# A gather of table rows by matmul, split in two exact float32r parts, with late gathers written out one by one, in a graph-network layer

## The reference

```python
xs = x[src]                                       # a row of x for each edge
deg_w = jnp.maximum(seg(edge_weights), 1.0)
deg_c = jnp.maximum(seg(jnp.ones_like(edge_weights)), 1.0)
norm = edge_weights / jnp.sqrt(deg_w[src] * deg_w[dst])
gcn = seg(norm[:, None] * xs) @ Wgcn + bgcn
sage = x @ Wsage_s + seg(xs) / deg_c[:, None] @ Wsage_n + bsage
agg_w = seg(edge_weights[:, None] * xs)
gin = ((1.0 + gin_eps) * x + agg_w) @ Wgin + bgin
gconv = x @ Wgc1 + agg_w @ Wgc2 + bgc
eop = seg(edge_weights[:, None] * jax.nn.relu(xs + edge_attr)) @ Wedge + bedge
out = layernorm(x + einsum('k,knd->nd', weights, stack([gcn, sage, gin, gconv, eop])))
```

## Time and profile before

| | |
|---|---|
| median of three runs | 2072.93 us |
| the profiled execution: span from first to last instruction | 2149.6 us |
| PE busy | 1612.0 us (75%) |
| POOL busy | 1416.1 us (66%) |
| DVE busy | 949.9 us (44%) |
| ACT busy | 868.5 us (40%) |
| mean granted TensorE clock | 0.891 |

### The profile page before, as it was taken

The page is one execution under the profiler, slowest core; times in us unless marked ns, Lnnn a source line. Parts: engine busy times, 40 slices in busy tenths (PEclk is TensorE's granted clock), DMA queues, the critical chain, the costliest instruction groups (busy, mean ns, idle before and its releaser), DMA issues.

```text
span 2149.6 us, 24142 instructions
## 1 busy us (share of the span) xinstructions
PE 1612.0 (75%) x6229; PEld 1037.0 (48%) x6229; DVE 949.9 (44%) x2579; ACT 868.5 (40%) x1181; POOL 1416.1 (66%) x1730
## 2 busy tenths in 40 slices
PE   2006577688889888888888988978988888888435
PEld 1005567545445454555455545545545455445335
DVE  7882465534334343443244433433435253334325
ACT  3784333334434252543254433533435253344003
POOL 6673766676676667667767666666666666666761
PEclk9999865889999899999899998989989999999757
DMA  5111433322222222222222222221222222212421
GB/s 98 25 25 46 132 106 100 83 44 47 58 51 61 48 47 58 52 48 58 44 66 49 55 60 44 54 51 43 68 48 47 54 57 47 59 43 56 103 44 37
DMA packets 81242, 124.52 MB, mean 58 GB/s; under 512 B 28856, under 2 KB 30631, under 8 KB 80009
## 3 DMA queue, kind: packets, MB, share of 16 engines
q0 software_dynamic: 44544, 48.32, 13.4%
q1 hardware_dynamic: 34966, 74.37, 10.9%
q10 hardware_dynamic: 1650, 1.04, 0.2%
HBM read 120.23 MB, written 3.40 MB: 58 GB/s over the span
## 4 chain that ended last, share of the span: by engine, by line
PE 40%; issue 20%; another core or an unknown queue 17%; DVE 11%; ACT 6%; POOL 3%; DVEq 2%; DMA 0%; POOLq 0%; SPq 0%; ACTq 0%
PE psum L1276 26%; PE psum L1257 11%; ACT ring L606 4%; POOL ring L564 3%; DVE ring L1072 2%; DVE sums L1061 2%; DVE early L986 1%; ACT early_x L687 1%; DVE attr L951 1%; DVE early L990 1%; PE psum L1308 1%; PE psum L1337 1%; PE psum L1338 1%; DVEq L1061 1%
## 5 line engine op out<-in xcount | busy, mean ns | idle before, releaser
L564 POOL DMA_INDIRECT ring<-node_table,idx x1280 | 1239.5, 968 | 612.4 <-issue 505.3
L1276 PE MATMUL psum<-table_sb,early_x 128*128 128x455 f32 x2464 | 1040.0, 572 | 46.5 <-issue 33.3
L1276 PEld LDWEIGHTS psum<-table_sb,early_x 128*128 128x128 f32 x2464 | 479.4, 200 | 531.2 <-issue 516.4
L1257 PE MATMUL psum<-ring 128*128 128x120 f32 x2560 | 412.5, 316 | 225.2 <-DVE ring L1072 104.7
L1257 PEld LDWEIGHTS psum<-ring 128*128 128x128 f32 x2560 | 378.3, 226 | 289.8 <-issue 160.1
L687 ACT ACTIVATE early_x<-early,minus_ids 128x256 f32<-128x256 f16 x616 | 408.1, 746 | 239.2 <-remote 144.6
L986 DVE TENSOR_TENSOR early<-psum,digit_hot 128x455 f32<-128x455 f32 x176 | 111.0, 631 | 885.4 <-remote 580.8
L678 ACT ACTIVATE early<-early 128x256 f32<-128x256 f32 x44 | 18.3, 416 | 523.4 <-DVE early L1007 305.0
L653 ACT ACTIVATE ring<-attr 128x512 f32<-128x512 f32 x160 | 99.6, 623 | 319.2 <-DVE attr L951 230.6
L690 ACT ACTIVATE early_x<-early_x,ones 128x1792 f32<-128x1792 f32 x88 | 157.4, 1789 | 2.9
L1257 PE MATMUL psum<-early 128*128 128x120 f32 x576 | 100.8, 328 | 75.8 <-issue 37.0
(11 more groups left out here) (156 smaller groups left out, 611.3 us busy)
## 6 DMA issues: line engine op xcount, KB each, us to landing
attr<-in_edge_attr SPq DMA_DIRECT2D x79, 512.0 KB
ring<-node_table,idx POOLq DMA_INDIRECT x1280
early<-in_edge_attr SPq DMA_DIRECT2D x36, 256.0 KB
src_all<-in_src SPq DMA_DIRECT2D x7, 1024.0 KB
early<-key_rows SPq DMA_DIRECT2D x11, 512.0 KB
early_x<-degree_rows SPq DMA_DIRECT2D x2, 1568.0 KB
early_x<-in_x,early_idx POOLq DMA_INDIRECT x112
node_table<-table_sb SPq DMA_DIRECT2D x1, 1666.0 KB, 6.1
```

The costliest lines, as they stand in the source:

```text
L564: nc.gpsimd.indirect_dma_start(out=feat[:, u, j, D:BLOCK], out_offset=None, in_=table, in_offset=bass.IndirectOffsetOnAxis(ap=idx[:, u, j: ...
L1257: last = nc.tensor.matmul(to[:, 0:3 * WINDOW], features[:, j, 0:2 * D], hots[:, j].rearrange("p k n -> p (k n)"), start=(j == 0), stop=(j ...
L1276: last = nc.tensor.matmul(pick_ps[k % 2].rearrange("p (b c) -> p b c", b=SPLIT), node_hot[:, k, a], table_sb[:, a * SPLIT:(a + 1) * SPLIT, ...
```

## The change

1. The node table is split by DVE into two parts whose sum is exactly the table: `table_hi` keeps each number's upper bits (the lower 12 are masked off), `table_lo` is the rest. Both, and the one-hot `node_hot`, are of type float32r. `pick_tile` issues 14 matmuls of 128x462 in place of seven of 128x455. 
2. `table_sb` no longer has its own memory: it lies in `sums[:, 1]`. So `sums[:, 1]` is set to zero only after the table is stored, split and lifted, and not at the start of the kernel.
3. The keys are stored tile by tile, so that ACT reads them for a tile as a row (`keys_of`), and the activation that makes them (L617) writes them in that order.
4. POOL's late gathers are written out as 160 times 8 instructions without a loop, and read their indices in `e_src`. The copies to `idx` and the waits for them are gone. 
5. The memory that the compiler is given for the descriptors of POOL's DMAs, `dynamic_dma_scratch_size`, is set to 4096 bytes of a partition; before, it was left at its default.

```diff
-        table_sb = sb("table_sb", [P, NT, TROW])
-
-        idx = sb("idx", [P, UNROLL, TILES], U32)
-
+        table_sb = sums[:, 1, 0:NT * TROW].rearrange("p (t d) -> p t d", d=TROW)
+        table_hi, table_lo = (sb(name, [P, NT, PART], F32R) for name in ("table_hi", "table_lo"))
+        top = ring[:, FEATS:FEATS + NT * PART].rearrange("p (t d) -> p t d", d=PART)
...
-        keys_of = [key_all[:, k * CHUNK:(k + 1) * CHUNK].rearrange("p (e j) -> p j e", j=TILES) for k in range(TURN_CHUNKS)]
+        keys_of = [key_all[:, k * CHUNK:(k + 1) * CHUNK].rearrange("p (j e) -> p j e", e=P) for k in range(TURN_CHUNKS)]
...
                 pool.wait_ge(table_stored, 16)
-                with pool.Fori(0, LATE_STEPS) as i:
-                    for u in range(UNROLL):
-                        it = v * LATE + i * UNROLL + u
-                        pool.wait_ge(gathered[u], (v * LATE_STEPS + i) * (16 * TILES))
-                        for j in range(TILES):
-                            if j % HALF == 0:
-                                tiles = slice(j, j + HALF)
-                                nc.gpsimd.tensor_copy(idx[:, u, tiles], e_src[:, bass.ds(i * UNROLL + u + BASE, 1), tiles].rearrange("p c j -> p (c j)")).then_inc(staged, 1)
-                                pool.wait_ge(staged, it * 2 + j // HALF + 1)
-                                if j == 0:
-                                    pool.wait_ge(chunk_product, it + 1)
-                                pool.sem_inc(gathers_begun, 1)
-                            nc.gpsimd.indirect_dma_start(
-                                out=feat[:, u, j, D:BLOCK], out_offset=None, in_=table,
-                                in_offset=bass.IndirectOffsetOnAxis(ap=idx[:, u, j:j + 1], axis=0),
-                            ).then_inc(gathered[u], 16)
+                for c in range(LATE):
+                    u = c % UNROLL
+                    if c >= UNROLL:
+                        pool.wait_ge(gathered[u], (v * LATE_STEPS + c // UNROLL) * (16 * TILES))
+                    pool.wait_ge(chunk_product, v * LATE + c + 1)
+                    pool.sem_inc(gathers_begun, 1)
+                    for j in range(TILES):
+                        nc.gpsimd.indirect_dma_start(
+                            out=feat[:, u, j, D:BLOCK], out_offset=None, in_=table,
+                            in_offset=bass.IndirectOffsetOnAxis(ap=e_src[:, c + BASE, j:j + 1], axis=0),
+                        ).then_inc(gathered[u], 16)
...
-            nc.scalar.activation(key_row16[0:BASE], key_row, ACT.Identity, bias=key_bias[0:BASE, 2:3]).then_inc(key_row_step, 1)
+            nc.scalar.activation(key_row16[0:BASE].rearrange("c (j e) -> c e j", e=P), key_row.rearrange("c (e j) -> c e j", j=TILES),
+                                 ACT.Identity, bias=key_bias[0:BASE, 2:3]).then_inc(key_row_step, 1)
...
-            nc.vector.memset(sums[:, 1], 0.0).then_inc(sums_zeroed, 1)
...
+            raw = table_sb[:, :, 0:PART]
+            link(nc.vector.tensor_scalar(top.bitcast(I32), raw.bitcast(I32), TOP_BITS, None, ALU.bitwise_and))
+            nc.vector.tensor_copy(table_hi[:, :, :], top).then_inc(table_split, 1)
+            nc.vector.tensor_tensor(out=table_lo[:, :, :], in0=raw, in1=top, op=ALU.subtract).then_inc(table_split, 1)
+            dve.wait_ge(table_split, 2)
+            dve.wait_ge(x_flip_used, NODE_GROUPS)
+            dve.wait_ge(table_stored, 16)
+            nc.vector.memset(sums[:, 1], 0.0).then_inc(sums_zeroed, 1)
             dve.wait_ge(sums_zeroed, 2)
-            dve.wait_ge(x_flip_used, NODE_GROUPS)
...
+                    pe.wait_ge(table_split, 2)
                     pe.wait_ge(early_added, v * EARLY + EARLY + 1)
                     pe.wait_ge(node_hot_made, v * (2 * UNITS) + n * 2 + k // 2 + 2)
                     pe.wait_ge(pick_taken, q + 1)
                     for a in range(SPLIT):
-                        last = nc.tensor.matmul(pick_ps[k % 2].rearrange("p (b c) -> p b c", b=SPLIT), node_hot[:, k, a],
-                                                table_sb[:, a * SPLIT:(a + 1) * SPLIT, 0:D + 1],
-                                                start=a == 0, stop=a == SPLIT - 1)
+                        for part in (table_hi, table_lo):
+                            last = nc.tensor.matmul(pick_ps[k % 2], node_hot[:, k, a],
+                                                    part[:, a * SPLIT:(a + 1) * SPLIT].rearrange("p b c -> p (b c)"),
+                                                    start=a == 0 and part is table_hi, stop=a == SPLIT - 1 and part is table_lo)
                     last.then_inc(picked, 1)
...
-    nc = bacc.Bacc("TRN2", target_bir_lowering=False, num_devices=1)
+    nc = bacc.Bacc("TRN2", target_bir_lowering=False, num_devices=1, dynamic_dma_scratch_size=4096)
```

More of the change, by code:

```diff
@@ L24 @@
 F32 = mybir.dt.float32
+F32R = mybir.dt.float32r
 BF16 = mybir.dt.bfloat16
@@ L59 @@
 BLOCK = D + TROW
+PART = D + 2
+TOP_BITS = -(1 << 12)
 BITS = WINDOW.bit_length()
@@ L178, in build @@
         inv_count = sb("inv_count", [P, NT])
-        table_sb = sb("table_sb", [P, NT, TROW])
-        idx = sb("idx", [P, UNROLL, TILES], U32)
+        table_sb = sums[:, 1, 0:NT * TROW].rearrange("p (t d) -> p t d", d=TROW)
+        table_hi, table_lo = (sb(name, [P, NT, PART], F32R) for name in ("table_hi", "table_lo"))
+        top = ring[:, FEATS:FEATS + NT * PART].rearrange("p (t d) -> p t d", d=PART)
+        assert NT * TROW <= SUMS and NT * PART <= HOTS
+        early_at = -(-nc.sbuf_base // 32) * 32
         early_flat = sb("early_x", [P, EARLY * TILES * D])
@@ L195, in build @@
         assert at_hots + HALF * HOT <= EARLY * TILES * D
-        node_hot = early_flat[:, at_hots:at_hots + HALF * HOT].rearrange(
-            "p (k a e) -> p k a e", k=HALF, a=SPLIT)
+        node_hot = nc.alloc_sbuf_tensor_at("node_hot", [P, HALF, SPLIT, P], F32R, offset=early_at + 4 * at_hots)
         root_src = sb("root_src", [P, TILES])
@@ L201, in build @@
         ends = np.cumsum(sizes).tolist()
-        sizes_g = (2 * HALF * BLOCK, 2 * HALF * D, HALF * 3 * WINDOW, 2 * SPLIT * (D + 1), CHUNK)
+        sizes_g = (2 * HALF * BLOCK, 2 * HALF * D, HALF * 3 * WINDOW, 2 * SPLIT * PART, CHUNK)
         early = sb("early", [P, max(ends[-1], sum(sizes_g), TURNS * CHUNK // 2)])
@@ L213, in build @@
         key_all = key_all.bitcast(F16)
-        keys_of = [key_all[:, k * CHUNK:(k + 1) * CHUNK].rearrange("p (e j) -> p j e", j=TILES) for k in range(TURN_CHUNKS)]
-        picks = picks.rearrange("p (s c b) -> p s c b", s=2, b=SPLIT)
+        keys_of = [key_all[:, k * CHUNK:(k + 1) * CHUNK].rearrange("p (j e) -> p j e", e=P) for k in range(TURN_CHUNKS)]
+        picks = picks.rearrange("p (s c b) -> p s c b", s=2, b=SPLIT)[:, :, 0:D + 1]
         kept = early[:, 0:TURNS * CHUNK // 2].bitcast(BF16).rearrange("p (k e) -> p k e", k=TURNS)
@@ L253, in build @@
         acc_e, root_ps = bank[7], bank[4]
-        pick_ps = [bank[k][:, 0:SPLIT * (D + 1)] for k in (4, 7)]
+        pick_ps = [bank[k][:, 0:SPLIT * PART] for k in (4, 7)]
         acc_g = bank[3]
@@ L294, in build @@
         root_in, root_out = sem("root_in"), sem("root_out")
-        table_ready, table_stored = sem("table_ready"), sem("table_stored")
+        table_ready, table_stored, table_split = sem("table_ready"), sem("table_stored"), sem("table_split")
         x_flipped, x_flip_used, ones_row = sem("x_flipped"), sem("x_flip_used"), sem("ones_row")
         node_product, node_taken = sem("node_product"), sem("node_taken")
-        staged = sem("staged")
         gathered = [sem(f"gathered{u}") for u in range(UNROLL)]
@@ L689, in hot_nodes @@
                     act.wait_ge(node_far, made + 1)
-                    nc.scalar.activation(to, to, ACT.Relu, bias=ones[:, 0:1], scale=-2.0).then_inc(node_hot_made, 1)
+                    nc.scalar.activation(to, to.bitcast(F32), ACT.Relu, bias=ones[:, 0:1], scale=-2.0).then_inc(node_hot_made, 1)
                 def turn(s, begun=True):
@@ L985, in pick @@
                         hot_c = digit_hot[:, bass.ds(c * TILES + half * HALF + k, 1), :].to_broadcast([P, D + 1, SPLIT])
-                        nc.vector.tensor_tensor(out=picks[:, k % 2], in0=pick_ps[k % 2].rearrange("p (b c) -> p c b", b=SPLIT),
+                        nc.vector.tensor_tensor(out=picks[:, k % 2], in0=pick_ps[k % 2].rearrange("p (b c) -> p c b", b=SPLIT)[:, 0:D + 1],
                                                 in1=hot_c, op=ALU.mult).then_inc(pick_taken, 1)
```

## The result

The changed kernel takes 1816.32 us (median of 4 runs, 1814.74 to 1816.7), the kernel before 2071.94 us on the same chip (4 runs, 2070.55 to 2073.82): a ratio of 0.8762 [0.875, 0.8775]. Its sign was right, its size was not: 1905 was forecast.

What follows compares the result with a forecast made beforehand. POOL's rate was taken as the late stage's bound: slots fall from 11.95 to 10.14 + 0.05 + 0.50 = 10.69 us, gaining 180 us; 2149.6 - 180 + 5 = 1975 us of span, times 0.9643 is 1905 us, range 1838 to 1998.

Steps and rivals of the forecast that it cites:

- POOL is the bound, and the copies are the gain: Late gathers: POOL needs 11.45 us a slot; removing two copies at 0.73 us each gives 209 us over 142.9 slots.
- 0.50 is my value between them, nearer the upper, since the size does fall: Late gathers: stalls for taking back descriptor memory rise from 0.13 to 0.50 us a slot, between bounds 0.13 and 0.77.
- eight gathers at their mean, slow ones included: 10.14: Late slot after the change: 8 x (0.968 + 0.30) = 10.14 us, before 0.05 us for its head.
- From slot 17 ... 11.95 each: Late gathers of the kernel before: 1707.8 us for 142.9 slots, 11.95 us each, the base of the gain.
- 34 us of waits: POOL's real waits for other engines in the kernel before; most would go, with 5 us put back in the sum.
- The early stage has no fetches and gains nothing: Slots before 17: PE with the chain through DVE and ACT binds at 12.5 us a slot, so gain 0.
- Table fetch on PE books nothing: float32r fetch: PE's six slots take 34 to 55 us, under POOL's 64.1, so nothing booked but the lost waits.
- Rival D: Table fetch: a float32r matmul is no cheaper than a whole fp32 one; at 0.76 us, near 2630 us; 3%.
- Rival B: Half the gain: clock stays low after the early stage, 2008 us, or slot's head costs 0.73 us, 1998 us; 9%.
- Rival C: Descriptor memory: room returns only after gathers land, 3.4 us a stall, 2148 us; 9% with everything down to no change.
- Rival A: Late gathers: stalls cost next to nothing more, no waits left, slot 10.27 us, gain 240, 1841 us; 13%.
- Pieces at the start: DVE's three new table-split instructions, about 2.1, 2.1 and 3.5 us, and the moved 5.3 us memset are hidden: 0.

Runs made afterwards that it cites:

- Experiment 3: Kernel before with only POOL's late gathers written out, no copies; fp32 fetch, old key order, default descriptor memory: 1814.54 us, ratio 0.8744.
- experiment 5: Late gathers written out, copies and waits kept: in the changed kernel 2096.7 us, ratio 1.0111; in the kernel before, default memory, 2073.59 us, ratio 1.0001.
- experiment 4: Changed kernel with the old gather loop, index copies and waits put back, 4096 bytes kept: 2097.42 us, ratio 1.0111.
- second profile: Kernel before, unchanged, profiled once more: one run of 2072.3 us, span 2070.5 us.
- experiment 8: Changed kernel with 30 picked chunks, four slots each, float32r fetch, and descriptor memory of 2048 bytes in place of 4096: 1756.58 us, ratio 0.8477.
- experiment 7: 30 picked chunks for 22, four slots each for six: in the changed kernel 1739.73 us; in the fp32-fetch kernel with only the gathers changed 2065.07 us.
- experiment 2: Kernel before with only the descriptor memory of POOL's DMAs set to 4096 bytes: 2102.21 us, ratio 1.0131.
- first profile: Execution of the unchanged kernel before whose trace the prediction was worked from: span 2149.6 us, where the runs take 2072.

## Why the prediction was off, point by point

**POOL is the bound, and the copies are the gain: right.** Experiment 3 shows that the gathers without copies give 0.8744, experiment 5 that the loop has no part in it, and experiment 4 that no other part of the change gives anything with the copies in place. The base slot of 11.45 us from parts was good too; the second trace has 11.48 us for a slot without a stall, 11.65 with its share of them.

**"0.50 is my value between them, nearer the upper, since the size does fall": this step failed, and it is the largest error.** I had read the stalls rightly as room taken back (their distance among the early gathers is 28 at 4096 bytes and 14 at 2048; at the default the first comes at gather 113), but taken for granted that they come wherever the memory has been filled. In the unbroken row of late gathers they don't come, at 4096 bytes or 2048 or at the default, but for the one at 113 and the single one of experiment 8. They show when POOL's row of gathers is broken, by waits for its copies (experiments 1, 5) or for PE (experiment 7, fp32). With the waits gone the 0.13 us a slot that they had cost went as well, and no 0.37 came: 0.50 x 142.9 = 71 us of the forecast's span. Even where the copies stay, the smaller memory costs 0.20 us a slot (experiment 2), not 0.37. That room is taken back in sixteens is wrong too, since 28 and 14 are no multiples of 16, and the upper bound of 0.77 was worked out from it. The estimate by the Trainium skill's figure (SBUF — State Buffer, SBUF size: 192, 224, or 256?) had a stall every 24 gathers; the measured distance is 28, and only among the early gathers.

**"eight gathers at their mean, slow ones included: 10.14", and 0.05 for the head: 0.17 us a slot too much.** Measured are 10.015, head and all. The mean of 968 ns belonged to the first profile; in the second it is 959. That is (10.19 - 10.015) x 142.9 = 25 us.

**"From slot 17 ... 11.95 each": the base was too slow.** In the second profile it is 11.65. This error was of the other sign: it promised (11.95 - 11.65) x 142.9 = 43 us of gain that there were not to be had. Bringing the span back by 0.9643 spread that over everything: the right ratio of a run to its own span is 2072.3 / 2070.5 = 1.0009. The 34 us of waits were part of the same execution; 5 us booked for them are 0.

**"The early stage has no fetches and gains nothing": wrong, 23 us.** From the first late gather to slot 17 there are 205.7 us before and 182.5 after (341.27 - 158.76). The step that failed is that PE was the bound there. With 17 x 11.65 = 198 us POOL by itself nearly filled that stage, and in the second profile it has no wait for PE but one of 0.9 us in the whole kernel. I had read 3.73 us for sixteen records as PE's need, but their length changes from moment to moment: in the changed kernel three groups of sixteen take 3.74, 2.25 and 2.05 us between 329 and 339 us.

After the change 17 slots at 10.0 would be 170 us, and 12 more are used. They aren't waits for PE or ACT either, since every gap ahead of these gathers but the first is the usual 0.30. They lie in the gathers themselves: of the first 136, the very first takes 3.91 us and 21 more take 1.14 to 1.60 us in place of 0.94. Of these 22, 15 start while DVE is at an instruction with two inputs in SBUF and four while it is at one with a single input (L832 or L972 of the changed kernel); all 19 end 0.8 us after that instruction. One of them, and DVE beside it:

```profile
227.96 1.48 POOL L562 DMA_INDIRECT ring<-node_table,e_src  x1 [0.30 <-issue]
227.94 0.68 DVE L956 TENSOR_TENSOR attr<-attr,ring 128x512 f32<-128x512 f32 x1
```

**Together**, against the second profile: 175 us of span promised; plus 71 (stalls), 25 (gathers and head), 5 (waits) and 23 (early stage), less 43 (base), less 1 at the two ends (the first gather is 2.1 us later, the tail 1.0 us shorter), make 255; measured are 2070.5 - 1814.9 = 255.6.

**Table fetch on PE books nothing: right,** and for the reason given. One matmul takes 0.212 us, between the bounds of 0.19 and 0.76 and near the lower. Rival D is out; "the change names it one pass", said against it, had no ground, since the change names only a type. Rival B named a clock that stays low after the early stage; it is 0.87 there, and that alone puts it out. (Experiment 3, where a whole fp32 fetch fits, has a clock of 0.99 and doesn't test it.) B's other way, 0.73 us at the slot's head, is out by the timeline, where that gap is 0.30. Rival C is out by the same rows as the 0.50. Rival A, no dearer stalls and no waits, 1841 us at 13%, was the closest. It kept the old stalls, the mean gather and an early stage without gain, and came out 25 us too high.

**Pieces at the start: nearly nothing, as booked.** The timeline of DVE in the changed kernel:

```profile
153.03 3.51 DVE L927 TENSOR_SCALAR ring<-sums 128x3234 int32<-128x3234 int32 x1
156.57 1.85 DVE L928 CAST table_hi<-ring 128x3234 fp32r<-128x3234 f32 x1
158.34 3.52 DVE L929 TENSOR_TENSOR table_lo<-sums,ring 128x3234 fp32r<-128x3234 f32 x1
...
180.03 5.32 DVE L933 MEMSET sums<- 128x6312 f32 x1 [18.17 <-issue]
```

8.9 us where I had 7.7, with 18 us of waiting left behind them. The subtraction lies just over the first late gather, which takes 3.91 us for it (158.76 above). The Trainium skill says in SBUF — State Buffer, Who interferes with whom, that a VectorE instruction with two inputs in SBUF contends with a GpSimd instruction that reads SBUF, and this row agrees: the gather reads its indices there, and ends 0.81 us after the subtraction. It is not the case of both shared ports that the prediction named. Under the first of the three, which has one input, two gathers took their usual 0.94 us (154.23 and 155.48). The keys' activation took 4.84 us where I had about 2. Nothing that bounds the time waits for it. The first late gather is 2.1 us later than before (158.76 against 156.62), and experiment 2 has the memory alone and nearly the same start: it is the stalls of the smaller memory that move it.

**What stays open.** Why the early gathers, which also follow each other without a break, do stall each time the memory is full, and the late ones don't. The two differ in the waits at a chunk's head, in their source and in their place in the program; no run separates these. Open too is what the single stall of 7.63 us in experiment 8 waits for, and why the first execution of the kernel before was 77 us longer than its runs.

## What to carry to other kernels

When an engine waits for its own instruction, count the wait and not the instruction: issued one group ahead, the same 320 copies cost about 0.1 us in place of 0.73 each. After an engine has been freed, move work onto it or off the new bound, since a faster instruction off the path shows nothing (float32r: 0 us with six slots, 325 us with four). Before a sum is made on a trace, hold its span against the runs; where they differ by 3.7%, as here, rates and waits of that trace aren't those of the runs.

## What was not expected of the hardware

- A float32r matmul of 462 columns starts every 0.212 us, an fp32 one of 455 columns is two records of 0.382: 3.6 times as long for one, 1.8 for the two exact parts that replace it.
- A stop of POOL costs more than its cause: besides the 0.63 us of each wait for its own copy, the stalls at gathers 225, 321, 417 and so on (1.54 us beyond the usual gap) come only in kernels in which POOL stops for a copy or for PE.
- Descriptor memory: 4096 bytes cost 28 us with the copies (ratio 1.0131) and nothing measurable without (1814.54 with the default and 1816.32 with 4096 bytes, in kernels that differ in the fetch as well), 2048 bytes 17 us with four slots, of which 10 are lost before slot 17 and 7 in one stall near the end.
- With a fetch nearly twice as long PE's granted clock was higher, 0.99 against 0.87 (stage of turns of experiment 3 and of the changed kernel), and the slots were as long, 10.03 and 10.01 us. No run separates what set the clock.
- A gather that POOL begins while DVE is at an instruction with two inputs in SBUF ends 0.8 us after that instruction: it takes 1.48 us in place of 0.94 beside one of 0.68 us, and 3.91 beside one of 3.52. With the waits gone, this is what the early stage of the changed kernel still loses.
